# A first attention with its loads, NF4 block scales and score bands put in another order, and two orders of the expert stage

## What is computed

```python
x = x + xattn0(layernorm(x), ctx)      # 8 heads of 16, band |i - j| <= 64 over 512 positions
x = x + ffn0(layernorm(x))             # silu(x w1') * (x w2'), then w3; w1, w2, w3 through NF4
x = x + xattn1(layernorm(x), ctx)      # 16 heads of 32
x = x + moe(layernorm(x))              # 32 experts, 6 per row, at most 192 rows each

def nf4_roundtrip(w):                  # blocks of 64 numbers
    scalers_1 = max(abs(blocks), axis=1)
    centered = scalers_1 - scalers_1.mean()          # the mean over one whole matrix
    qf = 128 / max(abs(centered), blocks of 64)
    scale = clip(round(centered * qf), -128, 127) / qf + scalers_1.mean()
    level = nearest(NF4, blocks / scalers_1)         # 16 levels
    return level * scale
```

## Time and profile before

| what | us |
|---|---|
| runs: median of 3 (lowest, highest) | 1548.79 (1542.08, 1549.16) |
| profiled execution, its own time | 1551.91 |
| profiled execution, span of its core | 1550.2 |
| busy in the span: PE, DVE, ACT, POOL | 1369.8, 1019.0, 768.9, 214.7 |

### The profile page before, as it was taken

How to read it: one execution, slowest core, us unless ns; L and a number is a source line. 1 busy time by engine, 2 the same in 40 slices (tenths; PEclk the granted TensorE clock), 3 DMA queues, 4 the chain that set the end, 5 groups by cost and what they waited for, 6 DMA issues and landing times. The chain is left out here.

```text
span 1550.2 us, 28462 instructions
## 1 busy us (share of the span) xinstructions
PE 1369.8 (88%) x8573; PEld 824.4 (53%) x8664; DVE 1019.0 (66%) x3300; ACT 768.9 (50%) x1721; POOL 214.7 (14%) x252
## 2 busy tenths in 40 slices
PE   1598999999998799999889999997689899999994
PEld 0254555555554544444455555553333577777682
DVE  4898999999996544646446777777578544544310
ACT  4966777777766533332166666665410033333221
POOL 2000000000000000000120000000100155555453
PEclk7689999999999999999999999998799999999997
DMA  8243343434320300000000000000600488898784
GB/s 295 69 110 95 82 115 85 109 96 106 99 71 9 123 0 0 0 0 1 27 15 15 15 14 14 14 1 1 233 27 28 133 245 244 252 258 253 211 262 78
DMA packets 72167, 147.43 MB, mean 95 GB/s; under 512 B 10644, under 2 KB 40180, under 8 KB 67872
## 3 DMA queue, kind: packets, MB, share of 16 engines
q1 hardware_dynamic: 59728, 116.77, 23.9%
q0 software_dynamic: 12368, 29.77, 9.1%
HBM read 112.16 MB, written 34.34 MB: 95 GB/s over the span
## 5 line engine op out<-in xcount | busy, mean ns | idle before, releaser
L361 ACT ACTIVATE probs_t<-ps_sc 128x512 f32<-128x512 f32 x256 | 152.3, 595 | 114.4 <-PE ps_sc L499 114.1
L741 DVE CUSTOM_DVE_ANT_0 masked_scores<-ps_max,band_mask 128x192 bf16<-128x192 f32 (+1 forms) x512 | 177.4, 383 | 19.7 <-PE ps_max L482 14.9
L1153 PE MATMUL f_ps<-f_xt,w_t 128*128 (+1 forms) x704 | 158.5, 379 | 4.8 <-DVE f_xt L1098 2.4
L2583 DVE TENSOR_TENSOR d_inter<-d_silu_g,d_su 128x384 f32<-128x384 f32 x32 | 17.7, 554 | 175.2 <-PE d_su L2304 170.3
L482 PE MATMUL ps_max<-k_stack,q_stack 96*128 96x192 bf16 (+1 forms) x512 | 95.8, 271 | 40.0 <-DMA k_stack<-dr_parts 18.2
L1736 ACT ACTIVATE c_probs<-c_s,c_negmax 128x128 f32<-128x128 f32 x256 | 90.4, 365 | 59.4 <-DVE c_negmax L1821 58.7
L356 ACT ACTIVATE nf_above<-nf_scaled,nf_sign_at 128x512 f16<-128x512 bf16 x165 | 115.7, 713 | 0.0
L1153 PEld LDWEIGHTS f_ps<-f_xt,w_t 128*128 128x128 bf16 x704 | 68.8, 98 | 87.4 <-issue 4.4
L482 PEld LDWEIGHTS ps_max<-k_stack,q_stack 96*128 96x128 bf16 x512 | 46.3, 100 | 113.0 <-issue 53.3
L2173 POOL DMA_INDIRECT out<-d_h,d_scatter_now x64 | 97.1, 1517 | 43.3 <-POOL d_scatter_now L2167 18.2
L499 PE MATMUL ps_sc<-q_stack,k_stack 98*128 98x256 bf16 x512 | 99.2, 275 | 3.8 <-issue 0.4
(11 more groups left out here) (334 smaller groups left out, 2747.9 us busy)
## 6 DMA issues: line engine op xcount, KB each, us to landing
d_wgu<-in_ex_gu SPq DMA_DIRECT2D x32, 1024.0 KB
d_wdown<-in_ex_d SPq DMA_DIRECT2D x32, 512.0 KB
dr_parts<-qk_parts SPq DMA_DIRECT2D x32, 384.0 KB, 4.8
q_stack<-dr_parts SPq DMA_DIRECT2D x32, 192.0 KB, 3.1
k_stack<-dr_parts SPq DMA_DIRECT2D x32, 192.0 KB, 3.4
out<-x_sb SPq DMA_DIRECT2D x17, 256.0 KB
nf_w<-in_nf_w POOLq DMA_DIRECT2D x3, 1408.0 KB, 15.2
q_stack<-dr_parts SPq DMA_DIRECT2D x32, 128.0 KB, 2.8
```

Of the source, the lines that this page charges most:

```text
L361: act.activation(pt[:, c, :], SP[c % 2][:].rearrange("p a w -> p (a w)"), ACT.Exp, scale=D0 ** -0.5).then_inc(s_e, 1)
L741: op = dve.tensor_tensor_reduce(masked[:, c % 2, k, off:off + hi - lo], M[c % 2][:, k, off:off + hi - lo], mask[:, k, off:off + hi - lo], ...
L1153: mm = pe.matmul(bank[:], w12[:, m, kt, ft * P:(ft + 1) * P], xt[:, q, kt, bass.ds(g * N, N)], start=(kt == 0 and q == 0), stop=(kt == KT ...
```

## The change

**Band.** `q_stack` loses its zero columns, and POOL no longer clears them. The scores of the first and the last key tile are computed over 192 columns, the mask over 448, and the exponentials over 448 (`kept`).

**Start.** DVE no longer waits for the weights; PE waits for three of them, and for the other four ahead of body 0. POOL loads the first NF4 matrix once the first piece of x is there, then two pieces of x, and, after the first and the second stack of group 0 have landed, the last piece of x and the other two matrices. The ones rows of `k_stack` are ACT's first instruction. The maxima of matrix 1 are taken ahead of the first `take_max`; those of matrices 2 and 3 in four halves in body 0, at steps 3 and 7 of each half. The scales are computed for one matrix in body 0 and for two in body 1; `nf4_weight` of the first two chunks waits for those of matrix 1 alone.

**Loop.** `max_rows` is split. SP sends the next batch's maxima out ahead of the stack load and fetches them behind it. On PE `max_t` and `pv` stand ahead of `o_back`.

**Experts.** POOL copies the index before it waits for the scatter before, and waits for each half apart. SP issues `d_wdown` of `e + 1` behind `d_wgu` of `e + 2`.

```diff
-    qst = sb("q_stack", [P, 2, H0, D + 2 * BAND], BF16)
+    qst = sb("q_stack", [P, 2, H0, D], BF16)
-    pt = sb("probs_t", [P, 8, 2 * WIN], F32)
+    pt = sb("probs_t", [P, 8, 2 * WIN - BAND], F32)
+    def kept(kp):
+        return (BAND, 2 * WIN) if kp == 0 else (0, 2 * WIN - BAND)
+    PIECES = [(0, 0, MNB, rises)] + [(m, lo, lo + MNB // 2, fold[:]) for m in (1, 2) for lo in (0, MNB // 2)]
...
 (SP, body)
+                if not final:
+                    max_out(1 - b, 0, 2 * i + 2)
+                if not last:
                     sp.wait_ge(s_s, 16 * i + 8)
                     load_stack(i + 2, b, 0, 8 * (i - b) + 32)
                 if not final:
-                    max_rows(i + 1, 1 - b, 0, 2 * i + 2)
+                    max_back(1 - b, 0, 2 * i + 2)
...
 (POOL)
+            pool.wait_ge(s_x[0], 16)
+            load_nf(0)
+            load_x(pool, 2)
+            load_x(pool, 3)
+            pool.wait_ge(s_am, 1)
+            gather_maxima(0, 1)
+            pool.wait_ge(s_ld[0], 96)
+            load_x(pool, 4)
+            pool.wait_ge(s_ld[0], 192)
+            load_nf(1)
+            load_nf(2)
+            pool.wait_ge(s_sc, 1)
+            spread_scales(0, 1)
+            pool.wait_ge(s_am, 5)
+            gather_maxima(1, 3)
+            pool.wait_ge(s_sc, 2)
+            spread_scales(1, 3)
...
 (ACT, body)
+                    if c in (2, 6) and first:
+                        magnitudes(1 if c == 2 else 2)
...
+                    if c in (2, 6) and first:
+                        magnitudes(3 if c == 2 else 4)
...
 (PE, scores)
-                pe.matmul(s[:], identb[:], mask[:], start=True, stop=False)
+                a, z = kept(kp)
+                pe.matmul(s[:].rearrange("p a w -> p (a w)")[:, a:z], identb[:],
+                          mask[:].rearrange("p a w -> p (a w)")[:, a:z], start=True, stop=False)
...
-                    mm = pe.matmul(s[:, k, :], kst[0:98, b, h, kt * P:(kt + 1) * P],
-                                   qst[0:98, b, h, kt * P:kt * P + WIN], start=False, stop=(k == 1))
+                    lo, hi, off = chunk_cols(kt)
+                    mm = pe.matmul(s[:, k, off:off + hi - lo], kst[0:98, b, h, kt * P:(kt + 1) * P],
+                                   qst[0:98, b, h, lo:hi], start=False, stop=(k == 1))
...
 (DVE, body)
+                    if c in (3, 7) and first:
+                        block_max(1 if c == 3 else 2)
                     if c == 5 and first:
-                        block_sums()
+                        block_scales(0, 1)
+                    if c == 5 and second:
+                        block_sums(1, 3)
+                        block_recip(1, 3)
...
 (POOL, scatter)
-                if not start:
-                    pool.wait_ge(s_sc, 32 * e)
                 pool.tensor_copy(sst[:, par, :], sidx[:, bass.ds(e, 1), :].rearrange("p o a -> p (o a)")).then_inc(s_sci, 1)
                 pool.wait_ge(s_sci, e + 1)
-                pool.wait_ge(s_yo, 2 * e + 2)
-                pool.wait_ge(s_o, 16 * (NB + 2))
-                pool.nop(nofuse=True)
+                if start:
+                    pool.wait_ge(s_o, 16 * (NB + 2))
+                else:
+                    pool.wait_ge(s_sc, 32 * e)
                 for a in range(2):
+                    pool.wait_ge(s_yo, 2 * e + a + 1)
+                    pool.nop(nofuse=True)
...
 (SP, experts)
-                for k in range(2 if last else 4):
+                for k in range(4):
                     e = 4 * q + k
-                    sp.wait_ge(s_um, e + 1)
-                    load_gu(sp, e + 2, k % 2)
-                    sp.wait_ge(s_dn, 2 * e + 2)
-                    load_down(sp, e + 2, k % 2)
+                    if not (last and k >= 2):
+                        sp.wait_ge(s_um, e + 1)
+                        load_gu(sp, e + 2, k % 2)
+                    if not (first and k == 0) and not (last and k == 3):
+                        sp.wait_ge(s_dn, 2 * e)
+                        load_down(sp, e + 1, (k + 1) % 2)
```

256 lines of the change are left out of this document (135 added, 121 removed).

## The result

In the series on record the changed kernel takes 1550.28 us (median of 12 runs, 1548.46 to 1554.65) against 1546.87 us of the kernel before (12 runs, 1541.26 to 1551.75): ratio 1.0036, 95% interval 1.002 to 1.0052. In a later series on one chip (run e12) it is 1550.47 against 1544.70 us, ratio 1.0032 [1.0014, 1.0051]. The forecast was 1529 us, 1515 to 1543, counted from the 1548.79 us that the first three runs of the kernel before gave. It was wrong, also in its sign.

A forecast was written before the change was run, and what follows sets the result against it. VectorE and TensorE were both taken as near full in the first attention, tied by two score buffers. Loop -13, start 0 and last stage -7 sum to -20 us, from 1548.79 to 1529 us, range 1515 to 1543.

The forecast's parts named there:

- Band: First attention's score steps: dropping padding saves 0.88 us of PE per batch, so DVE becomes the bound with 25.6 us.
- Orders in the loop: First attention's loop: new SP and PE orders remove PE's 0.5 us wait; gain 0.95 us per batch, 11.4 us over 12 bodies.
- Start: Up to the first body: first exponential at about 52.4 us, 12 us earlier; on DVE the shift is 13 us.
- Bodies: First loop bodies: folds and scales return, body 0 +5.9 us, body 1 +6.3 us; with body 2's wait +12.7 us.
- Rival C: Bodies 0 and 1: folds idle PE, its clock stays at the lower level; +4 us in all, 1553 us; chance 0.04.
- Root behind a second table load: ACT's start: second table load of 1.28 us ahead of the square root, no drain behind it; root at 10.9 us.
- Last stage: Experts' scatters and weight loads: 0.8 us saved at each of seven scatters, 5.6 us; with `d_wgu` 6.6, say 7 us.
- The 1 us for `d_wgu`: Last stage: SP asks for `d_wgu` before the `d_wdown` that blocked it; gain up to 1 us.
- B: Loop: DVE is the bound anyway, PE's saved columns become waits for `row_max`; 0.3 us per batch, 1537 us; chance 0.14.
- D: Start: loads out of order of need, second scales late, last x lands at 46; start +8, 1537 us; chance 0.15.

The follow-up runs named there:

- e12: The changed kernel itself, run again in a later series on one chip: 1550.47 us, ratio to the kernel before 1.0032.
- e17: e10 plus SyncE's new loop order (maxima sent out ahead of the stack load), wide band kept: 1536.27 us, ratio to the kernel before 0.9940.
- e1: Changed kernel with both loop orders undone (maxima out behind the stack load, `o_back` before `max_t` and `pv`): 1545.02 us, ratio to the kernel before 0.9991.
- e16: e2 with SyncE's loop order of the kernel before (maxima out behind the stack load): 1534.92 us, ratio to the kernel before 0.9921.
- e11: Changed kernel with `pv` ahead of `max_t` in the second half batch alone: 1544.01 us, ratio to the kernel before 0.9993.
- e2: Changed kernel with `pv` moved ahead of `max_t` in both half batches: 1535.41 us, ratio to the kernel before 0.9934.
- e5: e2 with the last quarter of x asked for earlier, between write and read of the maxima's round trip: 1533.10 us, ratio to the kernel before 0.9941.
- e14: e5 with the first maxima also sent out between batch 1's two stack loads: 1530.38 us, ratio to the kernel before 0.9900.
- e7: e2 without the block maxima of matrices 2 and 3 (four half folds and magnitudes left out): 1531.82 us, ratio to the kernel before 0.9932.
- e10: Kernel before with `pv` ahead of `max_t` in both halves, still behind `o_back`; nothing else of the change: 1543.78 us, ratio to the kernel before 0.9984.
- e15: e2 with the scatter order of the kernel before: 1537.76 us, ratio to the kernel before 0.9952.
- e9: e14's kernel with the block maxima of all three matrices back ahead of body 0: 1535.35 us, ratio to the kernel before 0.9936.

## Why the prediction was wrong, step by step

The sum by stages, in the two profiled executions:

| term | forecast | measured |
|---|---|---|
| up to the first body | -13 | -9.5 |
| body 0 | +5.9 | +7.8 |
| body 1 | +6.3 | +9.7 |
| bodies 2 and 3 | +0.5 | -2.0 |
| the other loop bodies | -11.4 | -0.5 |
| bodies 14 and 15 | -1.6 | -0.9 |
| feed-forward, second attention and what else lies between, not touched | 0 | -6.3 |
| last stage | -7 | -1.7 |
| sum | -20 | -3.4 |

The spans differ by 3.5 us; the rest is rounding.

**Band.** By the starts of the matmuls each piece was priced well. A mask starts 0.20 us before the next matmul and that one 0.19 us before what follows, for 0.22:

```profile
283.35 0.35 PE L522 MATMUL ps_sc<-band_mask,identb 128*128 128x448 bf16 x1
283.55 0.35 PE L527 MATMUL ps_sc<-q_stack,k_stack 98*128 98x256 bf16 x2
283.74 0.38 PE L573 MATMUL ps_nf<-nf_above,ident_f 128*128 128x512 f16 x1
```

The exponential takes 543 ns for 595. The step that failed is the next one, "DVE becomes the bound with 25.6 us": VectorE's 5.4 us wait for `ps_max` stayed, in a place where TensorE's own waits and its order, and not its columns, decide: e17 removes that wait without taking a column away.

**Orders in the loop.** With the band this is the largest miss, 11 us. Right was that TensorE's wait for the maxima goes, and e17 shows what that is worth with the wide band and `pv` ahead of `max_t` (0.53 us); beside the narrow band it would have gone anyway (e1, e16). Wrong was "On PE `max_t` and `pv` go ahead of `o_back`, which then finds `o_rows` done". `max_t(2i+2)` writes the bank that `o_norm` reads, and waits for the same `o_rows` as `o_back` did; `pv`, which waits for neither, was put behind it. The order of before had one instruction waiting there, and so has the new one. The kernel shows it: ahead of `max_t(2 * i + 2, 0)` stands `pe.wait_ge(s_on, 2 * i)`, and `o_back(i - 1)` begins with a wait for the same count of the same semaphore. The forecast also left the first half batch at "a part of the wait for `ps_max` stays", without asking what TensorE does between these two `smax`: that place held 0.56 of the 0.78 us (e11). e2, at 25.99 us, shows that most of the way to the forecast's 25.8 us was open, by an order that the change doesn't have.

**Start.** The chain up to 29 us came as forecast (root at 10.69, parts out at 18.73, landed at 22.78, second parts at 29.55). Behind that 3.5 us are lost, in two terms. The last quarter of x came at 42.35 and not at 40, and ScalarE's chain runs from there without a gap to the first exponential: 54.69 for 52.4, 2.3 us. The first row of maxima was forecast out near 40.6 and "PE ready at 48", and measured out at 40.45 and scores at 52.26. The forecast took the 2.7 us of the earlier trace rows for the way out, and it took 6.3 us beside a quarter of x; from the way back to the scores it took 5.5 us, beside 2.9 MB of NF4 weights that POOL asked for at 44.01. This second miss of 4.3 us used up the lead that TensorE was to have: VectorE starts its work of body 0 at 54.01, after 6.5 us of waiting for `ps_max`. e5 and e14 confirm it: x alone gave 1.6 us in the pair of e2 and e5, since the row of maxima then held the scores at 52.55; both together gave the scores at 47.99, as forecast, and the first exponential at 49.63.

**Bodies.** VectorE's work was sized right: 33.07 for 34.1 us in body 0, 31.06 for 31.5 in body 1, and e7 prices the folds at 8.7 us or more. (The working takes 5.3 us off body 0 for the scales, where its own rows give 4.7, and says of neither this nor the 5.9 us added to body 1 where the rest comes from; that was not what failed.) The waits around it were not: 5.4 us for 2.5, and 4.6 for 0.8. In body 1 they read so:

```profile
DVE masked_scores L775 <- PE ps_max L507: 3.9, 3, 2.0
```

TensorE's clock was 0.84 and 0.90 of full in the two bodies, between its two levels of 1.2 and 2.4 GHz, where body 1 of before ran at 1.00. Rival C had named this mechanism; its price, half clock through all of body 1, did not come. How much of the 4.6 us is the clock's, no run tells.

Body 2 waited 2.2 us for the second scales, where the forecast took 0.5, but VectorE's 5.5 us of waits for `ps_max` in bodies 2 and 3 of before fell to 0.7, and the two came out 2.0 us shorter.

**Root behind a second table load.** Right. ScalarE ahead of its first root:

```profile
0.83 1.28 ACT L347 ACT_TABLE_LOAD   x1 [0.83 <-PEq L2731]
2.12 7.02 ACT L347 ACTIVATE k_stack<-ones 2x8192 bf16<-2x8192 f32 x1
9.16 1.28 ACT L350 ACT_TABLE_LOAD   x1
10.46 0.20 ACT L350 ACTIVATE std<-eps 128x1 f32<-128x1 f32 x1
```

The next activation starts 1.30 us after the load began. The Trainium skill ("ScalarE: Activation LUTs", section "What ACT_TABLE_LOAD costs") has 1.38 us of drain beside the load; these rows leave no room for it, and the measurement decides.

**Last stage.** 0.28 us per scatter and not 0.8. Taking "0.8 us saved each" of the stretch between landing and issue for removable was the error; where the rest goes stays open. The 1 us for `d_wgu` was not tested by itself.

**The rivals.** The size of B for the loop ("PE's saved columns turn into waits for `row_max`") and the size of D for the start (+8, measured +6.0 up to the third x) both happened, and the last stage gave about a quarter of its term. B's mechanism did so only in part: TensorE's waits for `row_max` rose from 2.1 to 3.9 us in nine batches, its waits for `o_rows` and `x_sb` took 11.2, and "DVE is the bound anyway" is refuted by e2's 25.99 us. D's mechanism did not: the last x came at 42.35 and not at 46, and the second scales cost body 2 2.2 us; the start was lost mostly in waits inside bodies 0 and 1. They had been put as alternatives, each against a forecast that otherwise held, and the range reached to 1543 for each alone. They don't exclude each other: the loop and the start have nothing to do with one another. On the median of the kernel before in the series on record, 1546.87 + 6.0 for the start - 1.4 for the loop behind the third x - 1.7 for the last stage is 1549.8, and 1550.28 was measured. That it comes so close is in part luck: the stages between, which gave 6.3 us in the two profiled executions, and the last stage differ from one execution to the next by more than the gap. A range over alternatives has to hold their sum where they are independent.

## What to carry to other kernels

When an instruction is moved ahead of another because that one waits, look first at what the moved one waits for; if it is the same event, the wait has only changed its name, and an instruction that waits for nothing belongs in its place. Read the waits of the engine in the bound together with what its partner does in the microseconds before: time taken off a partner pays only in the steps where the partner is late, and there an order can be worth five times as much as less work (0.70 us by order, 0.13 by the narrow band together with the place of `o_back`). And before two gains are added, ask whether they remove one and the same wait. A small transfer that everybody waits for pays for whatever is in flight beside it, so its time in a quiet loop is no price for a busy start.

## What the runs showed of the hardware

Between the first attention and the last stage no line is changed, but the second attention took 304.7 us in the profiled execution of before, 298.8 in that of after, and 302.8 in another execution of the very same changed kernel (e12):

```profile
770.50:1075.20 304.70, 278.87 (x1670) 171.72 (x1684) 213.02 (x442) 199.63 (x730) 28.07 (x17) 0.97 0.05 15
```

```profile
775.30:1074.10 298.80, 276.79 (x1684) 169.77 (x1684) 217.57 (x442) 200.38 (x730) 28.13 (x17) 0.99 0.05 15
```

```profile
774.30:1077.10 302.80, 278.70 (x1670) 171.50 (x1684) 217.86 (x442) 200.41 (x730) 28.16 (x17) 0.97 0.05 15
```

The granted clock, 0.97, 0.99 and 0.97, goes with it. So it does with whole times: in the first series of the kernel before, the five runs at a mean clock of 0.953 took 1548.8 to 1551.8 us, the four at 0.957 or more 1538.4 to 1546.1. What starts such a stretch of low clock in the same code stays open. From the first weight turned to the last score matmul this stage took 302.8 to 304.1 us in the profiled executions of the kernels with the old start or its folds ahead of body 0, and 298.1 to 298.5 us in most of those with the new start, which would offset most of what that start costs (5.9 of 6.0 us between before and the changed kernel); but 301.2 in e7 and 302.2 in e12 and e15, which have it too, so the start is not the whole cause, and no run tells more. For the reader it means that one pair of profiles can miss the sign of a change of 0.3% by 6 us, and that the sum has to be made by stages.

An issue of SyncE's got shorter by where it writes: from 600 to 422 ns at the median for the loads into `q_stack` once that tile lost its padding, while `k_stack` kept its 423 and 420 ns. That had been no part of the forecast, and by the rows of e10 and e16 it is what took away the wait that SyncE's new order removes as well.

The same 384 KB of parts took 4.0, 5.3, 9.2 and 14.3 us to land (first parts of the changed kernel, its second, e5, e9), and the first 8 KB row of maxima 3.3 us (e14) or 6.3 us (the changed kernel) on its way out, for a median of 1.3 us over the bodies. e2 and e5 differ in nothing but when the last quarter of x is asked for: earlier, and the second parts take 9.2 us for 5.6 and the maxima 3.4 for 6.7.
